# Layer 0 of a two-layer convolution kernel: the forward patch transform as eight 64x32 tiles of the array, with the inverse transform in front of it

## What is computed

```
h = depthwise3x3(conv1x1(groupnorm(x)))           # 64 -> 384 channels
q, k, v = split(h, 3)                             # 128 channels each
out = irfft2(rfft2(q) * rfft2(k))                 # on patches of 8x8 pixels
out = layernorm over channels(out) * ln_w + ln_b
x = x + conv1x1(v * out) + b_proj                 # 128 -> 64 channels
```

## Time and profile before

| | us |
|---|---|
| three runs | 10979.61, 10986.28, 10986.41 |
| median | 10986.28 |
| the profiled execution, its own time | 10977.12 |
| its span | 10975.3 |

### The profile page before, as it was taken

One profiled execution on the slowest core, in us unless ns is written; L12 is line 12 of the kernel. 1 busy time (PEld: TensorE's weight loads), 2 busy tenths in 40 slices (PEclk: granted clock), 3 DMA queues, 4 the chain that ended last, 5 costly groups with the idle time before them and its releaser, 6 DMA issues. The chain is left out here.

```text
span 10975.3 us, 153647 instructions
## 1 busy us (share of the span) xinstructions
PE 9626.3 (88%) x52019; PEld 5638.5 (51%) x52150; DVE 7249.8 (66%) x7748; ACT 7053.3 (64%) x9174; POOL 5244.4 (48%) x2743
## 2 busy tenths in 40 slices
PE   0499999999999999999999999987777777777777
PEld 0266666666666666666666666642233333333322
DVE  4455555555555555555555555557999999999999
ACT  0377767777767777767777767722666666666666
POOL 0233433333433333433333443312777777777777
PEclk9999999999999999999999999998999999999999
DMA  9411112111112111112111112156222222222222
GB/s 194 103 43 43 43 44 51 43 43 43 43 43 51 44 43 43 43 43 50 45 43 43 43 43 49 46 137 153 69 68 62 68 68 64 66 68 67 64 68 68
DMA packets 559097, 673.51 MB, mean 61 GB/s; under 512 B 33206, under 2 KB 521180, under 8 KB 538268
## 3 DMA queue, kind: packets, MB, share of 16 engines
q1 hardware_dynamic: 559068, 673.15, 26.2%
HBM read 534.48 MB, written 138.55 MB: 61 GB/s over the span
## 5 line engine op out<-in xcount | busy, mean ns | idle before, releaser
L504 PE MATMUL banks<-w_hi,hi_lo 128*128 128x256 f16 x18432 | 2351.8, 273 | 53.3 <-DVE hi_lo L728 53.3
L504 PEld LDWEIGHTS banks<-w_hi,hi_lo 128*128 128x128 f16 x18432 | 1780.6, 98 | 462.1 <-ACT qk L619 206.1
L1113 POOL TENSOR_TENSOR prod<-prod 128x1024 f32<-128x1024 f32 x660 | 1672.5, 2534 | 531.2 <-DVE prod L1343 488.7
L462 POOL TENSOR_TENSOR u_im<-q_im,k_swap 128x512 f32<-128x512 f32 x512 | 700.8, 1369 | 2440.8 <-ACT q_im L637 2405.1
L737 DVE TENSOR_TENSOR u<-q_re,banks 128x512 f32<-128x512 f32 x512 | 351.1, 686 | 1892.6 <-ACT q_re L642 1478.1
L1153 PE MATMUL banks<-z,conv_w 128*128 128x512 f32 x3134 | 1579.4, 628 | 0.0
L1167 PE MATMUL banks<-kern_parts,sel 128*128 128x512 bf16 x2245 | 744.1, 410 | 820.4 <-DVE kern_parts L1329 470.4
L619 ACT ACTIVATE qk<-banks,inv_wscale 128x512 f32<-128x512 f32 x1024 | 689.7, 686 | 1072.7 <-PE banks L504 1060.0
L465 POOL TENSOR_TENSOR u<-u,u_im 128x512 f32<-128x512 f32 x512 | 650.3, 1270 | 932.8 <-DVE u L737 932.8
L521 PE MATMUL banks<-hi_lo,w_hi 128*128 128x512 f16 x4608 | 1081.0, 380 | 0.0
L1167 PEld LDWEIGHTS banks<-kern_parts,sel 128*128 128x128 bf16 x2376 | 188.8, 102 | 1663.6 <-DVE prod L1343 924.9
(11 more groups left out here) (184 smaller groups left out, 18997.5 us busy)
## 6 DMA issues: line engine op xcount, KB each, us to landing
xr<-in_x_dram SPq DMA_DIRECT2D x258, 640.0 KB, 8.2
xb<-y_scratch SPq DMA_DIRECT2D x268, 320.0 KB, 5.3
xa<-y_scratch SPq DMA_DIRECT2D x268, 256.0 KB, 4.0
out_dram<-res SPq DMA_DIRECT2D x260, 256.0 KB, 3.8
x_res<-in_x_dram SPq DMA_DIRECT2D x258, 256.0 KB, 4.1
xc<-in_x_dram SPq DMA_DIRECT2D x64, 1024.0 KB, 12.9
y_scratch<-ys SPq DMA_DIRECT2D x256, 256.0 KB, 4.1
yc<-y_scratch SPq DMA_DIRECT2D x256, 256.0 KB, 5.7
```

Source lines behind the costliest of these rows:

```text
L462: nc.gpsimd.tensor_tensor(u_im[:], q_im[:], k_swap[:], ALU.mult).then_inc(u_made, 1)
L504: r = pe.matmul(out, px, w, start=n == 0, stop=n == 13)
L1113: ins = nc.gpsimd.tensor_tensor(prod[0][:], prod[0][:], prod[n + 1][:], ALU.add)
```

## The change

- The forward transform becomes eight fp32 matmuls in place of two. Each takes 64 partitions (one of the two patches of a pixel tile, rows 0 to 63 or 64 to 127 of the array) and 32 columns of the array (real or imaginary part by which pair of pixel tiles), and streams 512 columns: q and k of two pixel tiles. Together they fill the 64x32 tiles of the array once. Patch 0 goes to bank 2, patch 1 to bank 3, and q and k lie there side by side; what reads q or k alone reads four blocks of 128 columns out of the two banks.
- `inverse` is issued in front of the forward transform, not behind it, and behind the waits for `k_read` and `q_split`. Its four outputs go to strided columns of its bank, so that the order of pixels is again that of v.
- The rows that are real alone lie now in two places of two partitions each, not in one place of four, so `freq_copy` ends with two copies in place of one; each moves two partitions.
- The three loads of `dft`, `idft` and `imag_sign` become 24 short ones in a new order of rows, and SP waits for all of them before it issues the transfers of v's rows.

The core of the diff:

```diff
-        dft = sb("dft", [P, P])
+        dft = sb("dft", [P, 2, 32])
...
-                     (dft[:], "dft"), (idft[:], "idft"), (imag_sign[:], "imag_sign"),
...
+                    for part in range(2):
+                        for half in range(2):
+                            for to, of, n in ((0, 2 * half, 2), (2, 4 + 30 * half, 30)):
+                                lo, src = C * part + 32 * half + to, C * part + of
+                                sp.dma_start(dft[C * half:C * half + C, part, to:to + n],
+                                             A["dft"][C * half:C * half + C, src:src + n]).then_inc(transforms_loaded, 16)
+                                sp.dma_start(idft[lo:lo + n], A["idft"][src:src + n]).then_inc(transforms_loaded, 16)
+                                sp.dma_start(imag_sign[lo:lo + n], A["imag_sign"][src:src + n])\
+                                    .then_inc(transforms_loaded, 16)
+                sp.wait_ge(transforms_loaded, 16 * 24)
...
+            b_qk, b_f, b_v, b_o, b_var, b_y = (bank[0], bank[1]), (bank[2], bank[3]), bank[4], bank[5], bank[6], bank[7]
+            freq = bank_pair[1][:].rearrange("p a (t c) -> p (a t) c", c=KQ)
+            b_q, b_k = freq[:, :, 0:P], freq[:, :, P:KQ]
+            by_block = lambda t: t.rearrange("p (g c) -> p g c", c=P)
...
-                    for t in range(4):
-                        px = slice(P * t, P * t + P)
-                        last = pe.matmul(b_o[:, px], u[:, px], idft[:], start=True, stop=True)
+                    by_patch = b_o[:].rearrange("c (half t p x) -> c p t half x", half=2, t=2, p=2)
+                    for p in range(2):
+                        for t in range(2):
+                            block = slice(P * (2 * p + t), P * (2 * p + t) + P)
+                            last = pe.matmul(by_patch[:, p, t], u[:, block], idft[:], start=True, stop=True)
                     last.then_inc(inv_done, 1)
+
+                def forward():
+
+                    for part in range(2):
+                        for half in range(2):
+                            for p in range(2):
+                                px, fr = slice(C * p, C * p + C), slice(C * part + 32 * half, C * part + 32 * half + 32)
+                                last = pe.matmul(b_f[p][fr, :], dft[px, part, :], qk[px, 2 * half:2 * half + 2, :],
+                                                 start=True, stop=True)
+                    last.then_inc(k_freq, 1)
...
                             pe.wait_ge(q_split, i * 8 + k)
-                        pe.matmul(b_q[:], dft[:], qk[:, :, 0:P], start=True, stop=True)
-                        pe.matmul(b_k[:], dft[:], qk[:, :, P:KQ], start=True, stop=True).then_inc(k_freq, 1)
-                        if not (first and k == 0):
                             inverse(i, k, not (first and k == 1))
+                        forward()
...
-                    act.copy(q_re[C:C + 4, :], b_q[C:C + 4, :]).then_inc(q_split, 1)
+                    act.copy(by_block(q_re[C:C + 2, :]), b_q[C:C + 2])
+                    act.copy(by_block(q_re[C + 32:C + 34, :]), b_q[C + 32:C + 34]).then_inc(q_split, 1)
```

More of the change, by code:

```diff
@@ L109, in build_program @@
             v_loaded = ph.enter_context(nc.semaphore("v_rows_loaded"))
+            transforms_loaded = ph.enter_context(nc.semaphore("transforms_loaded"))
             v_cleared = ph.enter_context(nc.semaphore("v_rows_cleared"))
@@ L124, in _ @@
                     sp.dma_start(dst, A[name]).then_inc(loaded, 16)
+                with nc.allow_non_contiguous_dma(reason="short rows of the transforms, once"):
+                    for part in range(2):
[8 more added lines that the diff above has]
+                sp.wait_ge(transforms_loaded, 16 * 24)
                 sp.wait_ge(turned, 16)
@@ L375, in build_program @@
             blk = ph.enter_context(nc.Block())
-            b_qk, b_v, b_q, b_k, b_o, b_var, b_y = (bank[0], bank[1]), bank[2], bank[3], bank[4], bank[5], bank[6], bank[7]
+            b_qk, b_f, b_v, b_o, b_var, b_y = (bank[0], bank[1]), (bank[2], bank[3]), bank[4], bank[5], bank[6], bank[7]
+            freq = bank_pair[1][:].rearrange("p a (t c) -> p (a t) c", c=KQ)
+            b_q, b_k = freq[:, :, 0:P], freq[:, :, P:KQ]
+            by_block = lambda t: t.rearrange("p (g c) -> p g c", c=P)
             def run(eng, body, tail=None):
@@ L633, in freq_copy @@
                         act.wait_ge(u_step, i * 8 + (k - 1))
[L634 to L639, removed]
+                    act.copy(by_block(k_swap[C:P, :]), b_k[0:C])
+                    act.copy(by_block(k_swap[0:C, :]), b_k[C:P]).then_inc(k_swapped, 1)
+                    act.activation(by_block(q_im[0:C, :]), b_q[C:P], ACT.Copy, scale=imag_sign[0:C, 0:1])
+                    act.activation(by_block(q_im[C:P, :]), b_q[C:P], ACT.Copy, scale=imag_sign[C:P, 1:2]).then_inc(q_im_ready, 1)
+                    act.copy(by_block(q_re[0:C, :]), b_q[0:C])
+                    act.copy(by_block(q_re[C:P, :]), b_q[0:C]).then_inc(q_copied, 1)
                     act.wait_ge(q_copied, i * 8 + k)
-                    act.copy(q_re[C:C + 4, :], b_q[C:C + 4, :]).then_inc(q_split, 1)
+                    act.copy(by_block(q_re[C:C + 2, :]), b_q[C:C + 2])
+                    act.copy(by_block(q_re[C + 32:C + 34, :]), b_q[C + 32:C + 34]).then_inc(q_split, 1)
                 def square(i, k, ring_used):
@@ L736, in product @@
                         v.wait_ge(inv_done, i * 8 + (k - 1))
-                    v.tensor_tensor(u[:], q_re[:], b_k[:], ALU.mult).then_inc(k_read, 1)
+                    v.tensor_tensor(by_block(u[:]), by_block(q_re[:]), b_k, ALU.mult).then_inc(k_read, 1)
                 def times_v(i, k, ring_used):
```

## The result

| | before | changed | ratio |
|---|---|---|---|
| median, us | 10986.35 | 11185.51 | 1.0182 (95%: 1.0164 to 1.0199) |
| lowest and highest | 10979.61, 10990.12 (4 runs) | 11183.15, 11186.74 (4 runs) | |
| profiled execution | 10977.12 | 11184.73 | |

The kernel is 199 us slower, where 103 us slower was forecast. The measured time lies in the range (11010 to 11290); the side was right and the loss about twice the forecast one, outside the bounds that the forecast itself was given (11063 to 11155).

What follows compares the result with a forecast made beforehand. TensorE bounds layer 0, with ACT, DVE and POOL close behind. Rounds 0.72 us longer, times 128, give 92 us; the weights block 10 and the tail 1 make 103 us, so 11089 us; range 11010 to 11290.

Steps and rivals of the forecast that it cites:

- The transform: TensorE's forward transform: eight tiles side by side take 1.10 us, with bounds of 1.02 and 1.88.
- row halves in turn: Rival, 10%: the array's two row halves take turns, so the transform takes 1.88 us; 11289 us in all.
- load that waits for its neighbour: Rival, 3%: a tile's load waits for its neighbour's matmul, making the transform 3.6 us; about 11970 us in all.
- One copy more: ACT's second short copy adds 0.59 us, gap included, ahead of the square and of the product.
- Steps 1 and 2: Start of the round: variance of k1 asked for at 19.33 us, waits until 20.25 for ACT's square, 0.92 us.
- Step 3: k1 to k2: inverse of k1 at 24.29 us, transform done at 26.37, first copy of k2 at 26.41.
- Step 4: k3: `u` ready at 51.79 us, TensorE there at 49.67, so it waits 2.2 us.
- The weights block: Loads before layer 0: 24 short issues and SP's wait for them add 7.9 to 12.7 us; 10 taken.
- the faster case: Rival, 5%: DVE's L771 no longer runs beside POOL's L452, and the k3 chain loses 2.36 us; 10810 us in all.
- the case of slack: Rival, 10%: the chains are 0.7 us a round shorter than summed, layer 0 ends level; 10997 us, no change.
- a granted clock below 1.00: Sign that the forecast is wrong: TensorE's clock granted below 1.00 in layer 0 behind the new waits.
- its tail: End of layer 0, a chain of all engines: one more copy and the later `k_freq` cost 1 us.

Runs made afterwards that it cites:

- e3: The kernel before with only the inverse moved in front of the two old forward matmuls: 11160.04 us, 1.0162 of before.
- e5: The changed kernel with DVE's three stack copies of k3 moved behind the product and the means: 10964.67 us, 0.9986 of before.
- e2: The changed kernel with the second of ACT's two short copies left out: 11033.53 us, 1.0048 of before.
- e4: The kernel before with one more short ACT copy, to a tile nobody reads, in front of the last one: 11017.74 us, 1.0032 of before.
- e6: The changed kernel with ACT's normalisation cut into two halves, one in front of the second qk_copy of k0: 11180.62 us, 1.0183 of before.
- e7: The changed kernel with the reorders of e5 and e6, and the 24 short loads behind the stores of zeros: 10819.99 us, 0.9851 of before.
- e1: The changed kernel with the forward transform in front of the inverse again: 10919.96 us, 0.9942 of before.
- e11: e6 with eight fp16 matmuls nobody reads in front of the inverse's wait in k3: 11076.72 us, 1.0087 of before.
- e12: The changed kernel with eight fp16 matmuls nobody reads in front of the inverse's wait in k3: 11204.09 us, 1.0184 of before.

## Why the prediction was right, and what it mis-sized

**Right, by its steps.** The bound: TensorE was all busy and still the change lost, since the chains of k1 and k3 were as near as 0.32 and 1.58 us. The transform: 1.09 us where 1.10 was taken, no row halves in turn, no load that waits for its neighbour (both rivals fall). One copy more: 0.58 and a gap, as taken. Steps 1 and 2: the variance of k1 at 20.36 from the start of `conv` (forecast 20.25), wait 0.94 (0.92). Step 3: inverse of k1 at 24.40 (24.29), transform done at 26.47 (26.37). Step 4: `u` for k3 at 52.12 (51.79), wait 2.41 (2.2). The weights block: 9.8 (10). L771, now L802, still takes 3.5 us beside POOL, so the faster case did not come; nor did the case of slack. What cost the time was not the work of TensorE but the order on the engines (e3, e5) and ACT's second copy (e2, e4).

**Mis-sized: the round.** Forecast 53.86, the round shown 54.45, mean of the rounds 54.62; against 53.15 that is 1.47 in place of 0.72, and 128 x 1.47 = 188 of the 199 us. The terms, for the round shown:

| term of the sum | taken | measured | more |
|---|---|---|---|
| start of `conv` of k0, over the normalisation L606 (now L636), to first copy of k1 | 14.73 | 14.84 | 0.11 |
| k1: first copy to end of transform, to first copy of k2 | 11.68 | 11.74 | 0.06 |
| first copy of k2 to `u` of k3 | 25.38 | 25.54 | 0.16 |
| `u` ready to start of inverse | 0.06 | 0.25 | 0.19 |
| inverse and transform to next `conv` | 2.01 | 2.08 | 0.07 |

These are 0.59 together, 76 us over 128 rounds. Every term was short by a little and none long, and they have no common cause. Beside the start of the inverse, the rows show L636 with 5.35 us where L606 had 5.26; ACT's first copy of k2 0.11 behind the transform's end, where 0.04 was taken; L802 with 3.52 where L771 had 3.46; 6.44 from its end to the start of the last three stack copies, where 6.35 was; and 1.06 from the start of the inverse to the transform, where 0.98 was taken from an inverse that waits for nobody. The largest term is the start of the inverse behind POOL. By the medians over the rounds it is 0.25 us in e2, e3, e5, e6 and e7 too, where TensorE had been idle for 0.86 us or more, and 0.05 in e1, e11 and e12, where it had been idle for 0.5. Idleness alone is not the reason: the variance of k1 starts 0.05 behind ACT's square, also after 0.97 us of idleness. What the 0.25 consists of was not measured apart.

**Missed: the half clock.** The text named a granted clock below 1.00 behind the new waits only as a sign of error, and priced it at nothing. It is 0.15 us a round, 19 us. What layer 0 lost beyond 128 times the round is 192.7 - 188 = 5 us, where 1 was taken for its tail.

So the mechanism was right and its size was half. The 103 us were the difference of two large numbers, 3.1 us waited and 2.4 saved a round, and 0.74 us that were not in it (0.59 of small terms, all on one side, and 0.15 of half clock) double it. That the measured time is in the range is luck: the range reached up to 11290 for the row halves that take turns, which fell; the forecast's own bounds end at 11155, 30 us short. (The lower of them, 11063, is 11066 by its own terms, 2 x 0.08 x 128 and 2 us off 11089; nothing rests on it.)

## What to carry to other kernels

Where one engine is busy all the time, ask how far behind it the others are, and at which instruction: work taken off it pays only as far as that, and an instruction that waits must stand behind all work that doesn't need to wait. Before moving something forward in a queue, compare the moment at which its input is ready with the new moment at which it is asked for; here the margin was 1.58 us and the move 1.71, and a wait in front of the next step's start is paid by all engines. Then loosen the chains by order alone (copies with a late due time behind work that others wait for, a long instruction cut where something short is due), which was worth nothing before and 2.3% together with the cheaper transform in front of the inverse.

## What was not expected of the hardware

- Behind a wait of 2.4 us TensorE's clock was granted at half for 3.4 us, in one round of ten in the changed kernel and in most rounds of e6, with waits of the same length (2.41 and 2.38 us). The length of the wait does not tell the rounds apart: in e6 it is 2.37 to 2.42 us where a stretch follows and 2.38 to 2.44 where none does. The moment at which the wait falls seems to: the stretches start at regular distances, 546.1 or 491.5 us in the changed kernel (ten or nine rounds), 54.6 or 109.2 in e6 (one or two). e2, with 1.8 us, had 12 such stretches, 587.1, 320.9 or once 853.3 us apart; e1, e3, e5 and e7, with 1.1 us or less, none.
- Eight fp32 matmuls in 64x32 tiles take 1.09 us together and one in the full array 1.02: the number of tiles costs 0.07 us.
- One DVE copy of the stacks runs long each round, the one that stands beside POOL's `u_im`: L718 with 1.67 us before, L747 with 1.90 in the changed kernel, where L749, the counterpart of L718, takes 0.69. The timelines of DVE in k2, before, and then changed:

```profile
3080.68 0.82 DVE L716 COPY hi_ind<-hi_all 64x2064 f16<-64x2064 f16 x1
3081.42 0.82 DVE L717 COPY hi_side<-hi_all 64x2064 f16<-64x2064 f16 x1
3082.25 1.67 DVE L718 COPY hi_side<-hi_all 64x2048 f16<-64x2048 f16 x1
```

```profile
3058.47 1.90 DVE L747 COPY hi_ind<-hi_all 64x2064 f16<-64x2064 f16 x1
3060.29 0.82 DVE L748 COPY hi_side<-hi_all 64x2064 f16<-64x2064 f16 x1
3061.12 0.69 DVE L749 COPY hi_side<-hi_all 64x2048 f16<-64x2048 f16 x1
```

POOL's row of that time in the changed kernel overlaps L747. In the kernel before, `u_im` ran from 3081.70 to 3083.37, beside L717 and L718. The copy that pays moved with it; that POOL is the cause was not tried by an experiment.

```profile
3058.25 1.43 POOL L482 TENSOR_TENSOR u_im<-q_im,k_swap 128x512 f32<-128x512 f32 x1 [3.78 <-ACT q_im L667]
```
